# Attention scores from a row's own four tokens on, in a permuted token order, with the diagonal squares completed by a turn

## The reference

```
score[i, j] = sum_c v[c] * tanh(p[i, c] + p[j, c])
x = x + softmax(score) @ n
```

## Time and profile before

| | |
|---|---|
| time, median of 3 runs | 12988.34 us (12986.25 to 12990.94) |
| the profiled execution | 12987.82 us, span 12986.1 us, granted TensorE clock 0.988 |
| PE busy | 12249.8 us (94%) |
| DVE busy | 11824.9 us (91%) |
| ACT busy | 11549.4 us (89%) |
| instructions | 298748 |

### The profile page before, as it was taken

The page is one execution under the profiler, slowest core; times in us unless marked ns, Lnnn a source line. Parts: engine busy times, 40 slices in busy tenths (PEclk is TensorE's granted clock), DMA queues, the critical chain, the costliest instruction groups (busy, mean ns, idle before and its releaser), DMA issues.

```text
span 12986.1 us, 298748 instructions
## 1 busy us (share of the span) xinstructions
PE 12249.8 (94%) x123504; PEld 5869.9 (45%) x123504; DVE 11824.9 (91%) x21373; ACT 11549.4 (89%) x7508; POOL 134.4 (1%) x93
## 2 busy tenths in 40 slices
PE   8999999999999999999578999999999999999999
PEld 3333333333333333333134555555555555555556
DVE  9999999999999999998998898888988889888881
ACT  8999999999999999998888888889888888888872
POOL 0000000000000000000000000000000000000000
PEclk9999999999999999999889999999999999999999
DMA  0000000000000000000101111111111111111113
GB/s 14 2 6 2 4 4 2 7 2 7 2 4 4 2 7 2 4 2 7 50 9 31 50 48 47 45 48 50 49 46 45 49 49 50 46 46 49 48 52 105
DMA packets 290051, 355.22 MB, mean 27 GB/s; under 512 B 28040, under 2 KB 242960, under 8 KB 288656
## 3 DMA queue, kind: packets, MB, share of 16 engines
q1 hardware_dynamic: 288656, 335.48, 8.8%
HBM read 314.14 MB, written 21.23 MB: 26 GB/s over the span
## 4 chain that ended last, share of the span: by engine, by line
PE 30%; DVE 15%; issue 4%; ACT 2%; DVEq 0%; ACTq 0%; POOLq 0%; POOL 0%
PE t_psS L939 11%; DVE t_ring L1330 10%; PE t_psC L896 9%; PE t_psS L907 4%; DVE t_ring L1334 2%; PE t_psF L767 1%; ACT t_ring L1028 1%; PE t_psB L824 1%; PE t_psF L736 1%; PE t_psB L855 1%; DVE t_side L1182 1%; DVE t_tok_after L1246 1%; DVE t_stats L1172 0%; PE t_psB L736 0%; PE t_psS L882 0%
## 5 line engine op out<-in xcount | busy, mean ns | idle before, releaser
L269 ACT ACTIVATE c_ring<-c_xn,c_w_neg 128x1568 f32<-128x1568 f32 x3824 | 5790.6, 1605 | 279.2 <-PE c_acc L228 272.9
L228 PE MATMUL c_acc<-c_ring,c_onehot 128*32 128x392 f32 x68608 | 5763.3, 493 | 136.3 <-DVE c_ring L424 79.2
L1028 ACT ACTIVATE t_ring<-t_ring 128x3136 f32<-128x3136 f32 (+4 forms) x2160 | 5138.6, 2403 | 549.6 <-DVE t_ring L1330 532.7
L1330 DVE TENSOR_SCALAR t_ring<-t_proj 128x784 f32<-128x784 f32 (+4 forms) x10240 | 4275.7, 488 | 560.4 <-PE t_psS L939 546.9
L416 DVE TENSOR_SCALAR c_ring<-c_xn,c_w 128x1568 f32<-128x1568 f32 x4752 | 4570.6, 1033 | 93.4 <-PE c_acc L228 93.3
L228 PEld LDWEIGHTS c_acc<-c_ring,c_onehot 128*32 128x32 f32 x68608 | 2217.9, 110 | 3655.6 <-issue 3203.7
L939 PE MATMUL t_psS<-t_ring,t_vhot 128*32 128x392 f32 (+3 forms) x36864 | 2839.4, 437 | 184.1 <-ACT t_ring L1028 157.2
L896 PE MATMUL t_psC<-t_filter_work 128*128 128x392 f32 (+3 forms) x6144 | 1644.7, 402 | 47.3 <-ACT t_filter_work L1015 47.2
L939 PEld LDWEIGHTS t_psS<-t_ring,t_vhot 128*32 128x32 f32 x36864 | 1027.6, 111 | 1245.3 <-issue 554.3
L896 PEld LDWEIGHTS t_psC<-t_filter_work 128*128 128x128 f32 x6144 | 1133.8, 192 | 711.8 <-ACT t_filter_work L1015 65.4
L424 DVE SCALAR_TENSOR_TENSOR c_ring<-c_xn,c_w,c_ring 128x784 f32<-128x784 f32 x1280 | 1265.8, 1031 | 97.7 <-ACT c_ring L269 96.3
(11 more groups left out here) (210 smaller groups left out, 3277.8 us busy)
## 6 DMA issues: line engine op xcount, KB each, us to landing
t_filter_work<-in_toep_dram SPq DMA_DIRECT2D x256, 393.0 KB, 3.4
t_filter_work<-mix_scratch SPq DMA_DIRECT2D x512, 192.0 KB, 2.4
t_filter_work<-in_toep_dram SPq DMA_DIRECT2D x256, 197.0 KB, 2.6
t_filter_work<-mix_scratch SPq DMA_DIRECT2D x512, 64.0 KB, 1.8
mix_scratch<-t_filter_work SPq DMA_DIRECT2D x4, 2048.0 KB, 9.5
c_xin<-in_x_dram SPq DMA_DIRECT2D x8, 784.0 KB, 4.3
x_scratch<-c_tmp SPq DMA_DIRECT2D x8, 784.0 KB, 3.5
t_proj<-x_scratch SPq DMA_DIRECT2D x16, 392.0 KB, 3.3
```

The costliest lines, as they stand in the source:

```text
L228: mm = pe.matmul(acc[32 * g:32 * g + 32, ch, 0:HALF], onehot[:, 31 - r:63 - r], ring[:, s % RING, g, ch * HALF:(ch + 1) * HALF], start=(s ...
L269: ins = act.activation(tile4(ring[:, s % RING, g, :]), window(xn, tap), ACT.Relu, bias=w0_neg[:, tap, 4 * r + g:4 * r + g + 1])
L1028: act.activation(ring[:, st % RINGS, 0:n], ring[:, st % RINGS, 0:n], ACT.Tanh).then_inc(th.s, 1)
L1330: dve.tensor_scalar(ring[:, st % RINGS, g * wd:(g + 1) * wd], proj[:, 128 * blk:T], proj[:, i:i + 1], None, ALU.add).then_inc(sums.s, 1)
```

## The change

Tokens 0 to 767 get a new order within their block of 128: token 4r+q stands at place 32q+r. The convolution stage writes x1 in this order, so that layer norms, softmax, experts and linear attention (with a permuted causal mask) work in it. So row r of the four quarters now holds four neighbouring tokens 4r to 4r+3. `proj` is put back into the natural order when ACT reads p from psF, and the spectral layer's input and residual when ACT reads them from psB (`in_order`, two instructions each in place of one).

A row group r then takes its columns only from 4r on (`pieces`; in block 5 all five groups of a step from the first one's 4r on), in the sums, the tanh and the matmuls. The diagonal square of a block comes out of psS with what is on and right of the 4 x 4 squares of its diagonal, and zeros left of them. `evac` takes it with a product by `half` (1, and 0.5 within the same four tokens) and puts the columns into the new order, in three instructions for blocks 0 to 4, two for block 5 and one for block 6. `fill` also turns the diagonal square itself, and `filled` adds the turned one to it. The fill of block 2 becomes two uses of psF (`fill2a`, `fill2b`) and its row maximum, exponential and scaling stand a slot later. The setup makes the permuted mask and `half`.

```diff
+BLOCKED = T // 128 * 128
+natural = lambda a: a.rearrange("p (q r) -> p r q", q=4)
+natural3 = lambda a: a.rearrange("p (t q r) -> p t r q", q=4, r=32)
...
-        tmp = sb("tmp", [128, 4, HALF])
+        tmp = sb("tmp", [128, 4, HALF]); x1o = sb("x1o", [128, 2, T])
...
-        if c == 0: wait(dve, s_st, 16 * d)
...
-        yield AT_OUT[c] + 4
-        k.sync()
-        dve.tensor_scalar(tmp[:, c, :], tmp[:, c, :], 1.0 / LEVELS, None, ALU.mult).then_inc(s_o, 1)
+        if h == 1:
+            yield AT_OUT[c] + 4
+            k.sync()
+            if im == 0: wait(dve, s_st, 16 * d)
+            both = tmp[:, c - 1:c + 1, :].rearrange("c h t -> c (h t)")
+            dve.tensor_scalar(natural3(x1o[:, im, 0:BLOCKED]), both[:, 0:BLOCKED].rearrange("p (t r q) -> p t r q", r=32, q=4), 1.0 / LEVELS, None, ALU.mult).then_inc(s_o, 1)
+            dve.tensor_scalar(x1o[:, im, BLOCKED:T], both[:, BLOCKED:T], 1.0 / LEVELS, None, ALU.mult).then_inc(s_o, 1)
     def tail(d): return [quant(d, c) for c in range(4)] + [result(d, c) for c in range(4)]
...
+def first_position(blk):
+    wd, n, w = width(blk)
+    return 512 - w if n == 2 else 0
+def pieces(blk, k):
+    wd = width(blk)[0]
+    out = []; o = 0
+    for r in step_rows(blk, k):
+        first = 4 * r if blk < 5 else 4 * PER_STEP[blk] * k
+        out.append((r, first, wd - first, o)); o += 4 * (wd - first)
+    return out
+def filled_at(blk, k):
+    r, first, w, o = pieces(blk, k)[-1]
+    return o + 4 * w
 def step_rows(blk, k):
...
-USES = ["fill2", "fill3", "pt2a", "pt2b", "out2", "fill4", "pt3a", "pt3b", "out3", "fill5", "pt4a", "pt4b", "out4", "pt5a", "pt5b", "out5", "pt6a", "pt6b", "out6",
+USES = ["fill2a", "fill2b", "fill3", "pt2a", "pt2b", "out2", "fill4", "pt3a", "pt3b", "out3", "fill5", "pt4a", "pt4b", "out4", "pt5a", "pt5b", "out5", "pt6a", "pt6b", "out6",
         "fill0a", "fill0b", "pt0a", "pt0b", "out0", "fill1a", "fill1b", "pt1a", "pt1b", "out1",
...
 AT_EVAC = 1
-AT_OLD = {2: dict(fill=0, rowmax=1, exp=2, scale=3, pt=4, out=8), 3: dict(fill=2, rowmax=3, exp=4, scale=5, pt=12, out=16),
+AT_OLD = {2: dict(fill=0, rowmax=2, exp=3, scale=4, pt=5, out=9), 3: dict(fill=2, rowmax=3, exp=5, scale=6, pt=12, out=16),
           4: dict(fill=10, rowmax=11, exp=12, scale=13, pt=20, out=24), 5: dict(fill=18, rowmax=19, exp=20, scale=21, pt=26, out=30), 6: dict(pt=32, out=36)}
...
         W(pool, ready, k, b)
         pool.tensor_tensor(rstd[:, :], var[:, :], half7[:, :], ALU.pow).then_inc(done.s, 1)
     pool.wait_ge(s_pc, 14)
+    for q in range(4):
+        pool.memset(S[:, q, 0:128], 1.0).then_inc(s_pc, 1)
+    pool.wait_ge(s_pc, 18)
+    for q in range(4):
+        pool.affine_select(out=S[:, q, 0:128].rearrange("p (q r) -> p q r", q=4), in_=S[:, q, 0:128].rearrange("p (q r) -> p q r", q=4), compare_op=ALU.is_ge, fill=0.0, base=127 * q, pattern=[[1, 4], [4, 32]], channel_multiplier=-4).then_inc(s_pc, 1)
     def one_pass(b, p, bb=None):
         if not no(b, 0):
...
             if h == 0: W(pe, lnB0, 1, i)
             bank(f"t{h}", b)
             transposes(lambda t: nrm[:, t, :], lambda t: psF[:, 128 * (t - 4 * h):128 * (t - 4 * h) + 128], s_fmade, parts[h])
-        for h in range(2):
+        for h, (lo, hi) in enumerate(WIDE):
             yield AT_NEXT["w"] + 2 * h
             bank(f"w{h}", b)
-            pe.matmul(psF[:, 0:HALF], wa[:, :], proj[:, HALF * h:HALF * (h + 1)], start=True, stop=True).then_inc(s_fmade, 1)
+            pe.matmul(psF[:, 0:hi - lo], wa[:, :], proj[:, lo:hi], start=True, stop=True).then_inc(s_fmade, 1)
...
         ins.then_inc(s_fmade, 1)
     def soft_old(blk, b, d, nrm):
         at = AT_OLD[blk]
-        if blk < 6:
+        if blk == 2:
             yield at["fill"]
-            W(pe, Sev, POS[blk] + 1, d)
-            fill(f"fill{blk}", blk, b, range(blk + 1, NT))
+            W(pe, Sev, scored(POS[blk]), d)
+            fill("fill2a", blk, b, range(2, 5))
+            yield at["fill"] + 1
+            fill("fill2b", blk, b, range(5, NT))
+        elif blk < 6:
+            yield at["fill"]
+            W(pe, Sev, scored(POS[blk]), d)
+            fill(f"fill{blk}", blk, b, range(blk, NT))
         yield at["pt"]
         W(pe, eP, blk + 1, d)
...
             for st, (blk, k) in enumerate(SLOTS):
                 buf = buffer_of(blk); pos = POS[blk]
-                if k == 0: W(pe, Sev, (-2, 0)[pos] if pos < 2 else pos - 1, b)
+                if k == 0: W(pe, Sev, (scored(4) - Sev.k, 0)[pos] if pos < 2 else scored(pos - 2), b)
                 wd, nch, w = width(blk)
-                rows = step_rows(blk, k)
+                at = 1024 * buf + first_position(blk)
                 W(pe, th, st + 1, b)
-                for n, r in enumerate(rows):
-                    for h in range(nch):
+                for r, first, wr, o in pieces(blk, k):
+                    for lo, hi in ((4 * r, w), (w, wd))[0:nch]:
                         for q in range(4):
-                            g0 = (q * len(rows) + n) * wd if blk == 5 else (4 * n + q) * wd
-                            ins = pe.matmul(psS[32 * q:32 * q + 32, buf, h, 0:w], vhot[:, 31 - r:63 - r], ring[:, st % RINGS, g0 + h * w:g0 + h * w + w],
+                            c = o + q * wr - first
+                            ins = pe.matmul(flatS[32 * q:32 * q + 32, at + lo:at + hi], vhot[:, 31 - r:63 - r], ring[:, st % RINGS, c + lo:c + hi],
                                             start=(r == 0), stop=(r == 31), skip_group_check=True)
...
             yield AT_NEXT["tev"] + 2 * h
             act.wait_ge(s_fmade, use(f"t{h}", b))
             act.activation(proj[:, lo:hi], psF[:, 0:hi - lo], ACT.Copy).then_inc(s_fread, 1)
-        for h in range(2):
+        for h, (lo, hi) in enumerate(WIDE):
             yield AT_NEXT["wev"] + 2 * h
             act.wait_ge(s_fmade, use(f"w{h}", b))
-            act.activation(proj[:, HALF * h:HALF * (h + 1)], psF[:, 0:HALF], ACT.Copy).then_inc(s_fread, 1)
+            if h: act.activation(proj[:, BLOCKED:T], psF[:, 384:hi - lo], ACT.Copy)
+            act.activation(proj[:, lo:lo + 384].rearrange("p (t r q) -> p t r q", r=32, q=4), natural3(psF[:, 0:384]), ACT.Copy).then_inc(s_fread, 1)
+    def in_order(dst, done):
+        act.activation(dst[:, 0:BLOCKED].rearrange("p (t r q) -> p t r q", r=32, q=4), natural3(psB[:, 0:BLOCKED]), ACT.Copy).then_inc(done.s, 1)
+        act.activation(dst[:, BLOCKED:T], psB[:, BLOCKED:T], ACT.Copy).then_inc(done.s, 1)
     def soft(blk, d, at):
         yield at["exp"]
         R = TOK_ROWS[blk]
...
             dve.wait_ge(s_mrun, i + 1)
     def evac(blk, b):
-        R = TOK_ROWS[blk]; wd, nch, w = width(blk)
+        wd = width(blk)[0]
         if blk < 5: dve.wait_ge(s_credit, NS * b + START[blk] + STEPS[blk])
         else: W(dve, pK, 1, b)
-        o = CORNER_AT if blk == 6 else 0
-        dve.tensor_copy(S[0:R, blk, 128 * blk:T].rearrange("p (h w) -> p h w", h=nch), psS[0:R, buffer_of(blk), 0:nch, o:o + w]).then_inc(Sev.s, 1)
+        if blk == 6:
+            dve.tensor_copy(S[0:TAIL, 6, BLOCKED:T], psS[0:TAIL, 1, 0, CORNER_AT:CORNER_AT + TAIL]).then_inc(Sev.s, 1)
+        else:
+            o = 1024 * buffer_of(blk) + first_position(blk); c0 = 128 * blk; c1 = c0 + 128
+            dve.tensor_tensor(natural(S[:, blk, c0:c1]), flatS[:, o:o + 128].rearrange("p (r q) -> p r q", q=4), half[:, :].rearrange("p (r q) -> p r q", q=4), ALU.mult).then_inc(Sev.s, 1)
+            if blk < 5: dve.tensor_copy(natural3(S[:, blk, c1:BLOCKED]), flatS[:, o + 128:o + BLOCKED - c0].rearrange("p (t r q) -> p t r q", r=32, q=4)).then_inc(Sev.s, 1)
+            dve.tensor_copy(S[:, blk, BLOCKED:T], flatS[:, o + BLOCKED - c0:o + wd]).then_inc(Sev.s, 1)
     def evacs(b):
         for blk in ORDER[:5]:
...
     def filled(name, blk, b, lo, hi):
         dve.wait_ge(s_fmade, use(name, b))
-        dve.tensor_copy(S[:, lo:hi, 128 * blk:128 * blk + 128], psF[:, 0:128 * (hi - lo)].rearrange("p (t c) -> p t c", c=128)).then_inc(s_fread, 1)
+        cols = slice(128 * blk, 128 * blk + 128)
+        o = 0
+        if lo == blk:
+            c.do(dve.tensor_tensor(S[:, blk, cols], S[:, blk, cols], psF[:, 0:128], ALU.add))
+            o = 128; lo += 1
+        dve.tensor_copy(S[:, lo:hi, cols], psF[:, o:o + 128 * (hi - lo)].rearrange("p (t c) -> p t c", c=128)).then_inc(s_fread, 1)
     def rowmax(blk, b, d, name):
         R = TOK_ROWS[blk]
-        W(dve, Sev, POS[blk] + 1, d)
+        W(dve, Sev, scored(POS[blk]), d)
...
     def soft_new(blk, b, tok):
         at = AT_NEW[blk]
         yield at["fill"] + 1
-        filled(f"fill{blk}a", blk, b, blk + 1, blk + 5)
+        filled(f"fill{blk}a", blk, b, blk, blk + 4)
         yield at["rowmax"]
-        filled(f"fill{blk}b", blk, b, blk + 5, NT)
+        filled(f"fill{blk}b", blk, b, blk + 4, NT)
+        c.sync()
...
         def body(step):
             dve.wait_ge(s_fread, use("w1", b - 1))
             for st, (blk, k) in enumerate(SLOTS):
```

(16 more changed lines are left out.)

62 lines of the change are left out of this document (41 added, 21 removed).

## The result

The changed kernel takes 12620.61 us (median of 4 runs, 12608.43 to 12622.34), the kernel before beside it 12987.81 us (4 runs, 12986.25 to 12990.94): a ratio of 0.9715 [0.9702, 0.9727], 367 us less where the forecast had 271 less. One execution in all of this, of the kernel where only the sums and the tanh narrow, took 16928.01 us at a granted clock of 0.694 and is left out.

A forecast was written before the change was run, and what follows sets the result against it. TensorE was taken to bound the fourteen steady passes except block 3, VectorE block 3 and the first two passes; -231 (fourteen times -16.5), -49 and +9 gave -271 on 12987.8, so 12717 us, range 12620 to 12820.

The forecast's parts named there:

- block 5 limited by TensorE's 19.3-0.5 = 18.8 of 20.6, so -1.8: Block 5 of a steady pass: TensorE's busy time in VectorE's 20.6 us stretch limits the gain to 1.8 us.
- Block 5's matmuls, 0.5 us by the weight loads: TensorE in block 5: 1740 fewer columns, 2.9 us at most, but weight loads limit the gain; 0.5 us taken.
- Blocks 4, 1 and 2 put down to TensorE alone: Steady pass: TensorE's column cost counts in these blocks, so each loses 3.25 us by its narrower matmuls.
- Added back, 1.1 + 0.5 + 0.3 us a pass: Steady pass: 1.1 us for six more transposes, 0.5 for the new hand-off, 0.3 for block 0's head.
- Blocks 1 and 2, 3.25 each: Steady pass: 1984 fewer columns a block on TensorE at 1.64 ns each, 3.25 us less in each block.
- The first two passes, -49: Passes 0 and 1, VectorE's: 28.3 us less work and 4.0 added in a pass, -49 us for both.
- Once, +9: Outside the passes: setup +3, convolution copies +4, the last image's softmax additions +2 us.
- the hand-off in the place of the wait for psC: Head of a pass: TensorE's new stall for block 2's split fill falls into the old 4.06 us wait; 0.5 us taken.
- B: Rival, 12608 us: a third of TensorE's 20 us idle a pass goes too, so a pass gains 24; chance 0.17.
- C: Rival, 12820 us: new hand-offs show, hopping copies cost double, fills come late; a pass gains 9.5; chance 0.20.
- E: Rival, 12898 us: narrower matmuls are not shorter; only block 3 and the first two passes gain; chance 0.05.
- D: Rival, slower: VectorE's evacuation pieces, hopping 32 elements, cost far over double; 13440 us at thirtyfold; chance 0.03.

The follow-up runs named there:

- the later fill: Changed kernel with the second part of block 2's fill, and what follows it for blocks 2 and 3, one slot later: 12636.97 us, ratio 0.9727.

## Why the prediction was wrong

The saving held: fewer columns, at the prices read from the rows, with the additions mostly hidden. One step of the sum failed, and smaller ones beside it, nearly all to the same side.

- **The step that failed: "block 5 limited by TensorE's 19.3-0.5 = 18.8 of 20.6, so -1.8".** Measured: -5.2 us a pass, so 14 x 3.4 = 48 of the 96 us missed. TensorE's busy time inside VectorE's stretch was read as a floor. With block 5's sums full and its matmuls narrow only 4 to 7 of its 100 us come; with the sums narrow and the matmuls full the stretch is 16.15 us long, with TensorE busy for all of it. The 19.3 us were what TensorE did while it waited for VectorE's block, part of it work that could as well stand in block 0's stretch.
- **Block 5's matmuls, 0.5 us by the weight loads.** Their busy time fell by 3.4 us. The loads were no limit, and the columns were miscounted: only the sums and the tanh of block 5 begin at the step's first 4r. Its matmuls begin at each group's own 4r (`for lo, hi in ((4 * r, w), ...)`), so 1984 columns go and not 1740, 3.25 us at 1.64 ns. It made little difference to the stretch: once the sums are narrow, the matmuls move it from 16.15 to 15.40. How much of block 0's further 2.7 us comes from them, no run parts.
- **Blocks 4, 1 and 2 put down to TensorE alone.** With only the matmuls narrow they gave 1.6, 2.3 and 2.3 us of the 3.25, though TensorE had been all but solid in 4 and 1. The rest came because VectorE's and ScalarE's columns went too, which the forecast did not say it needed; there its numbers were right, or too small, by luck.
- **Added back, 1.1 + 0.5 + 0.3 us a pass.** With nothing narrowed, transposes and hand-off showed in none of blocks 0, 1 and 2. What showed, 1.1 us a pass, was nearly all in VectorE's two stretches (0.6 in block 3, 0.4 in block 5), where the forecast had put 0.7, in block 3 alone. With these terms at nothing, the pass is 1.9 us shorter than forecast: 27 us.
- **Blocks 1 and 2, 3.25 each.** Measured 3.8 and 4.0. TensorE runs some four steps behind, so VectorE's stretch of a block holds the last, narrowest rows of the block before and all but the last of its own: (880 + 1512) x 1.64 = 3.9 us. This is argued and not shown: the same count gives 2.6 for block 4, where 3.2 were measured. It is worth 18 us.
- **The first two passes, -49.** Measured -55.6. The sums' term was right (-27.9 for -28.3) and the additions a little cheaper, and 5 us of waits went too. In pass 0 VectorE's waits for TensorE's score matmuls fell from 7.1 to 2.7 us, while its one wait for ScalarE stayed (7.8 and 7.9). No run parts this.
- **Once, +9.** Measured 8.8 before scoring and 2.0 in the tail.
- **Right as recorded:** 3.3 us a block on TensorE (3.7 and 3.6 in blocks 0 and 2), 1.64 ns a column; -28 us on VectorE and -39 on ScalarE; block 3 by VectorE, 3.5 for 3.6; the hand-off in the place of the wait for psC; the clock of the fourteen passes, 0.99; the hop hidden, though 1.7 times the price.

Of the rivals, B named 12608, the nearest number, but not by its mechanism: it wanted a third of TensorE's 20 us of idle gone, and 2 went. C (12820) and its showing hand-offs fall with the later fill and with the kernel where nothing is narrowed. E falls with the chain's 1.25 us and the matmuls-only kernel's 132 us. D falls with 1.80 ns a column. Block 5's term had no bound by VectorE alone: 7.0 us of sums for the 1.8, fourteen times, is 73 us more, three quarters of the way from the forecast to the range's low end.

## What to carry to other kernels

Where engines are joined by a ring of buffers, cut the pass into stretches and ask of each which engine is without a gap in it; the other engine's busy time in that stretch is no floor, since its work can slide over the borders (60 of 264 records did above; how far it can go, no run tested). A check is to narrow one engine's work alone and then the other's: read stretch by stretch, a gain that comes whole with one of them names the owner, and a gain that comes only with both means a shared one. And where the engine that owns a stretch is not the fullest of the pass, moving a little of its work to the emptiest engine there pays at once (58 us here for one row in eight of one block).
